# A recurrent layer with a mixture-of-experts block: context scan two tiles ahead, Wo bias preset, sorted top two

## What is computed

```python
xn = layernorm(x)
for t in range(S):                       # 128 steps, serial
    r = decay * r + ctx[:, t] * ctx[:, t]        # "context": squared and scanned
    retained = xn[:, t] * r
    inp  = retained @ Wi.T + bi
    gate = sigmoid(inp @ Wg.T + bg)
    state = tanh((gate * state + (1 - gate) * inp) @ A.T + inp @ Bm.T)
    out[:, t] = state @ Wo.T + bo
x = x + tanh(g_xattn) * out              # "residual"
fx = layernorm(x)
shared = swiglu(fx @ w_shared_in) @ w_shared_out
probs = softmax(fx @ w_gate + gate_bias) # "logits", 8 per token
top_val, top_idx = top_k(probs, 2)       # lowest index first where equal
hid = swiglu(fx @ w1_shared)
routed = sum(wdense[:, e:e+1] * (hid @ w2[e]) for e in range(8))  # wdense: top_val at top_idx, else 0
x = x + tanh(g_ffn) * (shared + routed)
```

## Time and profile before

| | us |
|---|---|
| median of 3 runs | 529.41 (528.71 to 534.01) |
| profiled execution, its own time | 534.36 |
| its span, first to last instruction | 532.1 |
| PE busy | 494.0 (93%) |
| DVE busy | 436.9 (82%) |
| ACT busy | 216.6 (41%) |
| POOL busy | 174.8 (33%) |

### The profile page before, as it was taken

The page is one execution under the profiler, slowest core; times in us unless marked ns, Lnnn a source line. Parts: engine busy times, 40 slices in busy tenths (PEclk is TensorE's granted clock), DMA queues, the critical chain, the costliest instruction groups (busy, mean ns, idle before and its releaser), DMA issues.

```text
span 532.1 us, 12569 instructions
## 1 busy us (share of the span) xinstructions
PE 494.0 (93%) x4506; PEld 369.6 (69%) x4506; DVE 436.9 (82%) x1382; ACT 216.6 (41%) x500; POOL 174.8 (33%) x261
## 2 busy tenths in 40 slices
PE   5978677999999999999999999999999999979986
PEld 4865566776867776767768777767678687747552
DVE  3788849788898978888898989888888978797976
ACT  4566564443533434434434335344444343322120
POOL 3021564432324233233323243332433243241330
PEclk8999788999999999999999999999999999989999
DMA  6751011020202020110202020301220101000001
GB/s 158 228 165 35 1 36 26 2 61 22 60 22 59 10 69 0 47 32 20 59 20 59 20 59 0 73 5 36 43 59 1 41 1 42 1 20 1 22 1 39
DMA packets 46062, 22.05 MB, mean 41 GB/s; under 512 B 35664, under 2 KB 39376, under 8 KB 46032
## 3 DMA queue, kind: packets, MB, share of 16 engines
q1 hardware_dynamic: 45904, 21.65, 15.8%
q0 software_dynamic: 128, 0.00, 0.1%
HBM read 17.45 MB, written 4.19 MB: 41 GB/s over the span
## 4 chain that ended last, share of the span: by engine, by line
PE 59%; DVE 23%; issue 6%; ACT 5%; POOL 1%; DVEq 0%; ACTq 0%
PE bank L459 22%; PE bank L470 21%; PE rec L459 8%; DVE r L1115 3%; PE rec L484 3%; ACT c L788 3%; DVE x L1167 2%; DVE acc L1095 2%; DVE u_full L1079 2%; PE rec L489 2%; DVE c_turned L1108 2%; DVE u_hi L1077 2%; PE bank L528 1%; PE bank L747 1%; DVE ret L1128 1%
## 5 line engine op out<-in xcount | busy, mean ns | idle before, releaser
L777 ACT ACTIVATE state<-rec 128x64 f32<-128x64 f32 x128 | 36.7, 286 | 177.8 <-PE rec L489 177.5
L470 PE MATMUL bank<-w_hi,hid_hi 128*128 128x512 f16 x256 | 97.8, 382 | 8.8 <-DVE x L1167 5.0
L470 PE MATMUL bank<-w_hi,hid_lo 128*128 128x512 f16 x256 | 97.8, 382 | 0.0
L470 PE MATMUL bank<-w_lo,hid_hi 128*128 128x512 f16 x256 | 97.7, 382 | 0.0
L1077 DVE SCALAR_TENSOR_TENSOR u_hi<-gt,state 128x64 f16<-128x64 f32 x127 | 36.4, 286 | 52.3 <-ACT state L777 52.0
L1098 DVE SCALAR_TENSOR_TENSOR acc<-bank,wts,acc 128x256 f32<-128x256 f32 x128 | 62.0, 484 | 4.5
L1095 DVE SCALAR_TENSOR_TENSOR acc<-bank,wts,acc 128x256 f32<-128x256 f32 x128 | 60.8, 475 | 1.8 <-PE bank L470 1.6
L484 PE MATMUL rec<-u_hi,a_hi 128*128 128x32 f16 x512 | 47.6, 194 | 10.5 <-DVE u_hi L1077 9.6
L484 PEld LDWEIGHTS rec<-u_hi,a_hi 128*128 128x128 f16 x512 | 38.0, 98 | 24.8 <-DVE u_hi L1077 18.5
L1482 POOL TENSOR_TENSOR cn_lo<-cn,cn_hi 128x512 fp32r<-128x512 f32 x14 | 17.9, 1276 | 102.4 <-ACT cn_hi L840 102.4
L470 PEld LDWEIGHTS bank<-w_hi,hid_hi 128*128 128x128 f16 x256 | 25.0, 98 | 33.1 <-DVE x L1167 6.5
(11 more groups left out here) (228 smaller groups left out, 1460.9 us busy)
## 6 DMA issues: line engine op xcount, KB each, us to landing
x_sb<-in_x_dram SPq DMA_DIRECT2D x16, 256.0 KB, 3.2
c_sb<-in_ctx_dram SPq DMA_DIRECT2D x64, 64.0 KB, 2.8
xr_sb<-in_x_dram SPq DMA_DIRECT2D x16, 256.0 KB, 3.3
out_dram<-acc SPq DMA_DIRECT2D x16, 256.0 KB, 2.5
raw_w<-in_L_ffn_w_dram SPq DMA_DIRECT2D x8, 256.0 KB, 4.4
raw_sh<-n_L_ffn_w_shared_in_dram SPq DMA_DIRECT2D x1, 512.0 KB, 6.2
raw_w<-in_L_ffn_w_shared_dram SPq DMA_DIRECT2D x1, 512.0 KB, 6.6
raw_Wi<-in_L_xattn_Wi_dram SPq DMA_DIRECT2D x1, 256.0 KB, 3.3
```

The source lines that it names most:

```text
L470: last = pe.matmul(dst, a[:, kc, s * P:(s + 1) * P], w(part, kc), start=first, stop=(kc == KC - 1 and a is a_lo), skip_group_check=True)
L777: act.activation(step_of(state[i % 2], t), step_of(rec[i % 2], t), ACT.Tanh, scale=1.0 / PSCALE).then_inc(st_ready[t], 1)
```

## The change

Four edits:

1. **Context two tiles ahead.** `context_turned` and `context_squares` keep their place in the round but work on tile f instead of a; `scanned` moves from between steps 1 and 2 (tile a) to between pairs 2 and 3 of step 6 (tile f). `retained` stays, and finds its scan done in the round before. The context is loaded one round earlier. Round 1, which did none of this, now does it for tile 3.
2. **Wo bias.** POOL's `residual` is gone. ACT copies the scaled bias into the Wo bank (`wo_preset`, 128x512, between `hs_hi` and the tanh of step 1), PE's Wo product adds onto it, and waits for it. Once at the start, bo is scaled on DVE, and Wo is turned with plain matmuls.
3. **Logits with tokens on partitions.** The activations are the stationary side and the gate weights (16 columns) the moving one: 8 matmuls of 16 columns for 4 of 256. The 4 transposes go.
4. **Sorted top two.** DVE's `max` sorts the 8 logits of a token (after `hs`, end of the round), `max_index` gives their places; a comparison with the expert numbers makes two one-hot rows (`hot`), which are weighted and added. `more`, `same`, `lmax` and POOL's five rank operations go.

The core of the diff (declarations of tiles and semaphores left out):

```diff
@@ SP
+            sp.wait_ge(turned, 2)
+            load_c(3, first)
...
                 m = i + 3
                 if k.has(m):
                     sp.wait_ge(xn1_ready, k.n(m - 2))
                     load_x(m, k)
-                m = i + 2
                 if k.has(m):
                     sp.wait_ge(turned, k.n(m - 2))
                     load_c(m, k)
@@ PE
                 recurrence(i, 1, k)
                 if k.has(c):
-                    if k.has(d):
-                        pe.wait_ge(sil_w_ready, k.n(d))
+                    pe.wait_ge(wo_bias, k.n(c))
                     pe.wait_ge(st_hi, k.n(c))
                     pe.wait_ge(st_lo, k.n(c))
                     for s in range(HALVES):
                         last = token_product(bank[B_WO][:, s * D:(s + 1) * D],
-                                             lambda part, kc: split["wo"][part][:, kc, :], st_s[c % 2], s, s == 0)
+                                             lambda part, kc: split["wo"][part][:, kc, :], st_s[c % 2], s, False)
...
-                    for kc in range(KC):
-                        for v in xn2_s[c % 2]:
-                            last = pe.matmul(bank[B_LG][:, 0:TOK], wgate_s[:, kc, :, :].rearrange("p g e -> p (g e)"),
-                                             v[:, kc, :], start=(kc == 0 and v is xn2_s[c % 2][0]),
-                                             stop=(kc == KC - 1), skip_group_check=True)
+                    for s in range(HALVES):
+                        for kc in range(KC):
+                            for v in xn2_s[c % 2]:
+                                last = pe.matmul(bank[B_LG][:, s * 2 * E:(s + 1) * 2 * E], v[:, kc, s * P:(s + 1) * P],
+                                                 wgate_s[:, kc, :], start=(s == 0 and kc == 0 and v is xn2_s[c % 2][0]),
+                                                 stop=(kc == KC - 1 and v is xn2_s[c % 2][1]), skip_group_check=True)
                     last.then_inc(lg_done, 1)
@@ ACT
+            def wo_preset(c, k):
+                if not k.has(c):
+                    return
+                if k.static and c == 0:
+                    act.wait_ge(setup_dve, 11)
+                if k.has(c - 1):
+                    act.wait_ge(sil_w_ready, k.n(c - 1))
+                act.copy(bank[B_WO][:, :].rearrange("p (s d) -> p s d", s=HALVES),
+                         bo_fold[:, :].unsqueeze(1).to_broadcast([P, HALVES, D])).then_inc(wo_bias, 1)
...
                     act.wait_ge(hs_ready, k.n(d))
                     act.copy(flat(hs_s[0][:, :, :]), flat(hs[:, :, :])).then_inc(hs_hi, 1)
+                wo_preset(c, k)
 
                 tanh_step(i, 1, k)
                 if ahead:
                     gate_tanh(a, k)
-                else:
-                    context_squares(a, k)
+                context_squares(f, k)
                 bias_set(a, k)
@@ DVE
-                if not ahead:
-                    context_turned(a, k)
+                context_turned(f, k)
 
                 gated_state(i, 1, k)
                 if ahead:
                     blend(a, k)
-                if not ahead:
-                    scanned(a, k)
                 if not ahead:
                     retained(a, k)
...
                 if k.has(d):
-                    dve.wait_ge(lg_ready, k.n(d))
-                    dve.tensor_reduce(lmax[:, :], lg[:, :, :], AX_X, ALU.max).then_inc(lmax_ready, 1)
...
-                    dve.tensor_tensor(more[:, :, :, :], others, mine, ALU.is_gt)
-                    dve.tensor_tensor(same[:, :, :, :], others, mine, ALU.is_equal).then_inc(same_ready, 1)
+                    dve.wait_ge(top_ready, k.n(d))
+                    dve.tensor_tensor(ld[:, :, :], top[:, :, :], top[:, :, 0:1].to_broadcast([P, HALVES, E]),
+                                      ALU.subtract).then_inc(ld_ready, 1)
+                    for n in range(HALVES):
+                        last = dve.max_index(top_at[:, n, :], top[:, n, :], lg[:, n, :])
+                    last.then_inc(top_at_ready, 1)
                 add_pair(5, e, k)
                 if k.has(d):
-                    dve.wait_ge(lmax_ready, k.n(d))
-                    dve.tensor_tensor(ld[:, :, :], lg[:, :, :], lmax[:, :].unsqueeze(2).to_broadcast([P, HALVES, E]),
-                                      ALU.subtract).then_inc(ld_ready, 1)
+                    dve.wait_ge(top_at_ready, k.n(d))
+                    dve.tensor_copy(chosen[:, :, :], top_at[:, :, 0:2]).then_inc(chosen_ready, 1)
...
+                    for n in range(HALVES):
+                        last = dve.tensor_tensor(hot[:, n, :, :], experts[:, :].unsqueeze(1).to_broadcast([P, 2, E]),
+                                                 chosen[:, n, :].unsqueeze(2).to_broadcast([P, 2, E]), ALU.is_equal)
+                    last.then_inc(hot_ready, 1)
...
-                    dve.scalar_tensor_tensor(out=flat(picked[:, :, :]), in0=flat(rank[:, :, :]), scalar=2.0,
-                                             in1=flat(ex[:, :, :]), op0=ALU.is_lt, op1=ALU.mult).then_inc(picked_ready, 1)
+                    for n in range(HALVES):
+                        last = dve.tensor_tensor(hot_w[:, n, :, :], hot[:, n, :, :],
+                                                 ex[:, n, 0:2].unsqueeze(2).to_broadcast([P, 2, E]), ALU.mult)
+                    last.then_inc(hot_w_ready, 1)
+                    dve.wait_ge(hot_w_ready, k.n(d))
+                    dve.tensor_tensor(picked[:, :, :], hot_w[:, :, 0, :], hot_w[:, :, 1, :], ALU.add).then_inc(picked_ready, 1)
...
                 add_pair(2, d, k)
+                scanned(f, k)
                 add_pair(3, d, k)
...
-                    for g in range(BLOCKS):
-                        last = dve.transpose(lg_t[32 * g:32 * (g + 1), :, :], product[32 * g:32 * (g + 1), :, g, :])
...
+                    for n in range(HALVES):
+                        last = dve.max(top[:, n, :], lg[:, n, :])
+                    last.then_inc(top_ready, 1)
@@ POOL
-            def residual(i, k):
-                pool.wait_ge(xr_in[i % 2], k.dma(i))
-                for s in range(HALVES):
-                    last = pool.tensor_tensor(xr_sb[i % 2][:, s * D:(s + 1) * D], xr_sb[i % 2][:, s * D:(s + 1) * D],
-                                              tgbo[:, :], ALU.add)
...
-                    pool.tensor_tensor(b4[:, :, :], b8[:, :, 0:4], b8[:, :, 4:8], ALU.add).then_inc(b4_ready, 1)
...
-                    pool.tensor_tensor(flat(rank[:, :, :]), b2[:, :, 0], b2[:, :, 1], ALU.add).then_inc(rank_ready, 1)
```

98 lines of the change are left out of this document (33 added, 65 removed).

## The result

The changed kernel takes 515.02 us (median of 4 runs, 513.36 to 515.61) against 531.26 (528.71 to 534.01) for the kernel before in the same session: ratio 0.9666, 95% interval 0.9626 to 0.9705. The forecast was 516.5 us. The profiled execution takes 515.2 us by its own time, span 513.4, at a mean granted clock of 0.977 (before: 534.36, 532.1, 0.973). In both, the clock granted to TensorE is 1.00 (2.4 GHz) through all of rounds 3 to 14, so these can be laid side by side. Outside them it isn't the same: from 50 us on it is 0.50 (1.2 GHz) from 56.1 to 62.9 and 73.2 to 80.0 us after, and from 56.2 to 63.0, 73.2 to 76.6, 90.3 to 93.7 and 476.0 to 479.4 us before. The lines L484, L489, L470, L1077, L1082, L1167 of before are L480, L485, L466, L1088, L1093, L1178 now.

What follows compares the result with a forecast made beforehand. PE was taken as the bound, waiting for a late `x1`: 12 rounds x (0.99 + 0.21) = 14.4 us, less 1.5 at the start, is 12.9; 529.41 - 12.9 = 516.5 us, from 513.5 to 519.5 (8 in 10: 513 to 527.5).

Steps and rivals of the forecast that it cites:

- What bounds the kernel: PE sets the time; between steps 3 and 4 pair 0 waits for a late `x1`, 0.99 us a round lost.
- I find no other gap in PE's starts in a round: In a loop round PE loses time only ahead of pair 0, so its floor is 28.42 us.
- nothing on the path: End of round on DVE: dropping the logits' 4 transposes, 1.05 us ahead of 0.6 us of idleness, gains nothing.
- Edit 3 on PE: Logits matmuls on PE: 0.44 us become 0.23, gaining 0.21 us in every round.
- rival 2: Sorting on DVE: each MAX and MAX_INDEX takes 1.3 us, total 538 us; 9%, shared with other slowdowns over 1%.
- POOL's rank work was beside everything: nothing: Taking the rank operations of the top-two choice off POOL gains no time.
- Start: Rounds 1 and 2: squares of tile 3 delay the tanh, 1.5 us lost in sum, from 0 to 3.
- End: Last three rounds, where DVE leads and small operations change places: 0 us, from -1 to +1.
- Level: Forecast subtracts 12.9 us from the 529.41 us median, taking the profiled run's extra 4.95 us as a first execution's.
- Rival 1: Last `u_lo` waits behind POOL's `st_lo`, 0.84 us a round; both rounds 526.6 us, 19%; one 521.5 us, 13%.

Runs made afterwards that it cites:

- the four with a memset: Changed kernel plus a spare DVE memset: 128x128 ahead of the last u 518.01 us, behind the sorts 515.00; 128x256 ahead 524.22, with `st_lo` waiting 516.22.
- the kernel with the wider memset: Changed kernel plus a spare 128x256 DVE memset ahead of the round's last u: 524.22 us; with `st_lo` waiting for the last `u_lo`, 516.22 us.

## Why the forecast came out right, and where it was wrong

By stretches of the trace, with each edit undone on its own (differences to the changed kernel, us; they don't add, since two kept gains can hang on one condition). The last column says little by itself: among the changed kernel and the four with a memset, which are alike up to round 3, it begins between 112.96 and 114.00 us.

| | rounds 3-14 | round 15 to the end | start of round 3 |
|---|---|---|---|
| all four (before) | +15.86 | +3.51 | -0.67 |
| edit 1 | +15.32 | +0.28 | -1.10 |
| edit 2 | +15.14 | +2.37 | -0.11 |
| edit 3 | +5.85 | +0.61 | -0.46 |
| edit 4 | +1.72 | +1.99 | -2.31 |

- **What bounds the kernel**: right. PE's chain, broken by the late `x1`. In the table of steps, 2-3 and 3-4 together gain 0.98 us, 0.99 forecast.
- **Edit 1**: right down to its times, in the rounds of the loop. Counted from step 1 of the round, `u_hi` of step 3 stood at 4.66 in the forecast and 4.72 in the trace, `x1` at 5.31 and 5.40. `hot` was held by `hid_lo` as foreseen; in the loop's other round `chosen` was held in its place, 1.10 us, and it came to the same. Counted from step 6: scan 2.41 and 2.42, pair 3 3.68 both, `u_lo` 5.08 and 5.06, POOL's `st_lo` 5.13 and 5.11.
- **"I find no other gap in PE's starts in a round", and for edit 3 "nothing on the path"**: wrong. There was a second gap of 0.12 to 0.15 us behind step 0, where the transposing of x waited for `hs`, and `hs` stood behind the transposes of the logits. It makes 1.8 of the 15.86 us. I had searched the chain of waits for pieces of other engines, and a gap this small doesn't break the chain; only start-to-start differences against a like step show it.
- **Edit 3 on PE**: 0.23 us a round, 0.21 forecast.
- **Edit 4**: the time of the sorts was right (0.2 taken; 0.23 for two `MAX8`, 0.24 for a search's two instructions where starts are 0.15 apart), so rival 2 had nothing. "POOL's rank work was beside everything: nothing" was wrong once the scan was gone: 0.08 to 0.23 us a round, and 2 us at the end. The two errors, here and at edit 3, were of one kind and both made the forecast gain too small.
- **Edit 2**: "nothing" is right of the copy in the rounds of the loop; PE waits for it three times in the whole span, 0.9 us together. I had named what the residual's going frees, one `u_lo`, but left out of the sum that the whole of edit 1 hangs on it. The run without it shows 15 us in the rounds. The forecast took no harm from this, since all four edits were made together.
- **Start**: +0.67 us, +1.5 forecast, and like kernels differ by up to 1.04 us there, so the +0.67 may be nothing. The tanh of step 2 came 2.37 us late, 2.5 forecast. Round 1 as a whole lost 2.1 and round 2 gave back 1.6, 1.0 forecast, but this is not the mechanism of the forecast alone: 1.1 us are the late tanh (step 2-3), another 1.1 the step 6-7 of round 1, where the granted clock is 0.50 for 6.8 us instead of 3.4, and round 2 gains because the stretch at 0.50 that the kernel before has there (90.3 to 93.7 us) is missing. Two of the kernels with a memset have their low stretches where the kernel before has them, and take 28.4 and 28.6 us for round 1 instead of 30.05, and 30.05 for round 2 instead of 28.87.
- **End**: -3.5 us, where I took 0, from -1 to +1: the term that was furthest off. Two things were left out. DVE leads there, so what DVE or POOL no longer do can count: with edit 4 undone 2.0 us come back, as waits of PE for DVE. And the granted clock: 1.48 us of the 3.5, as shown above. With edit 2 undone 2.4 us come back (in round 15, step 4-5 takes 5.02 and 5-6 5.13 us where the changed kernel has 3.85 and 4.23), but 1.65 of them are again a stretch at 0.50, from 477.2 to 480.6 us, and only 0.4 a `u_lo` of round 15 that the residual holds. All four traces with the residual have such a stretch in round 15, and none of the ten without it; what brings it about no run shows.
- **Level**: I subtracted from a median of 529.41 us; the later sessions put the kernel before at 531 to 534. The gain was 16 to 18 us, not 12.9. The time of 516.5 was near partly because a gain too small was taken from a level too low, which is luck. Nor was the 4.95 us of the profiled execution a first execution's extra: of the 35 later executions of the kernel before, the seven with a mean granted clock of 0.973, as the profiled one has, took 533.9 to 534.6 us, and the seven with 0.985 or 0.986 took 528.6 to 533.0. And the bounds of start and end add up to 2.5 us to either side, 514 to 519, not to the 3 us that I wrote.
- **Rival 1**, that `st_lo` gets in front of `u_lo`: it didn't happen in the trace, by the 0.05 us forecast in one of the loop's rounds and by 0.02 in the other. I had put my error at 0.1 us, so that it came out on the good side was luck in part. As a mechanism it is shown: four kernels met it (with the residual, with edit 1 alone, with each of the two memsets ahead of the last u), and a wait that fixes the order takes it away. Its price is 0.97 us a round where `u_lo` is held, 1.30 where `u_full` is and 1.46 where `u_hi` is, 0.84 forecast. The 0.13 us between 0.84 and 0.97 are a matter of reading: I took the moment at which w1 wants pair 4 from the chain of waits, whose pieces begin 0.16 us later than the matmuls' starts in the timeline (step 0 at 252.09 in the chain above, 251.93 in the timeline).

What stays open: why the other four executions of the kernel without edit 4 take 3 to 4 us more than the profiled one (their mean granted clock is 0.972 to 0.979, its own 0.990, but no trace shows where they lose the time); and what sets the stretches at 0.50. The changed kernel with `st_lo` made to wait, and no memset, was not run.

## What to carry to other kernels

Where two engines can hold each other up, write down the margin between the starts of each such pair, not only the busy times: here 0.02 us of DVE's start decided about 0.97 us a round, the changed kernel itself has no more than that to spare in every other round, and an edit that was worth 13 us in company (528.29 against 515.02) cost 10 us alone (543.47 against 533.71). Where the order matters and the late one has slack, fix it by a semaphore; the kernel with the wider memset took 28.15 us a round with the wait and 29.04 without. And don't judge an edit as "off the path" by the kernel before if another edit of the same change takes away what made it so. And before a difference at the start or the end of a trace is put down to an edit, lay the granted clock of the two stretches side by side.

## What the runs showed of the hardware

- An operation of DVE that reads two tiles of SBUF and starts while POOL's subtraction runs ends 0.02 to 0.13 us behind POOL's end, whatever its size: `hot` took 1.10 us instead of 0.26, `ld` 1.09 instead of 0.27, `u_full` and `u_lo` 1.23 instead of 0.27 and 0.23. Operations that read one input from PSUM weren't held: `acc` 0.47 us beside the residual's `xr_sb` (251.57), `retained` 0.75 for two beside `hid_lo` in the kernel before. In the other direction POOL's operation took 1.19 to 1.24 us instead of 1.16 when it started up to 0.06 us behind DVE's `u_lo`. That is 0.03 to 0.08 us more, though 0.16 to 0.23 us of `u_lo` still lay ahead, so POOL wasn't held for the whole of the 0.23 us that the trace gives for `u_lo`.
- I hadn't expected it of `chosen`, a conversion of 4 elements with one input in SBUF: 1.11 us under `hid_lo`, 0.16 where it starts 0.01 us ahead of it. The Trainium skill, page "SBUF — State Buffer", section "Who interferes with whom", names `cast` among the operations that can take the port pair that both engines share; that agrees with this 1.11 us. Its rule that the order of issue decides who blocks agrees with the two `u_lo` 0.01 us to either side of `st_lo`, 0.23 and 1.23 us.
- Eight matmuls with 16 columns take 0.18 us in the chain, against 0.23 for eight with 32: half the columns take off about a fifth.
- 24 matmuls of 256 columns took 5.01 us at a granted clock of 0.50 (75.23 in the changed kernel) and 2.64 us at 1.00.
